# Routing and expert products of a gated cross-attention and expert kernel: GpSimd takes over normalising and adding, products leave PSUM in fours

## The reference

```
for layer in (0, 1):
    x = x + tanh(g_xattn[layer]) * attention(layernorm(x), ctx, ctx [, mask])
    x = x + tanh(g_ffn[layer])   * experts(layernorm(x))
# experts, layer 0 (512 hidden features an expert):
    g = softmax(x @ gate_w);   top 2 of 8, divided by their sum
    y[e] = gelu(x @ w1[e] + b1[e]) @ w2[e] + b2[e];   out = sum over the top 2 of g * y
# experts, layer 1 (64 hidden features an expert):
    g = sigmoid(x @ gate_W) * route_scale;   top 2 of 8, divided by their sum
    the same, plus a shared expert gelu(x @ Ws1 + bs1) @ Ws2 + bs2
```

## Time and profile before

| | |
|---|---|
| median of three runs | 1082.89 us |
| the profiled execution | 1076.07 us, its span 1074.2 us |
| busy: PE / DVE / ACT / POOL | 940.6 / 770.7 / 587.4 / 459.4 us (88 / 72 / 55 / 43%) |
| chain that ended last | PE 63%, DVE 20%, ACT 8%, issue 5%, SP queue 2% |
| mean granted TensorE clock | 0.973 |

### The profile page before, as it was taken

How to read it: one execution, slowest core, us unless ns; L and a number is a source line. 1 busy time by engine, 2 the same in 40 slices (tenths; PEclk the granted TensorE clock), 3 DMA queues, 4 the chain that set the end, 5 groups by cost and what they waited for, 6 DMA issues and landing times.

```text
span 1074.2 us, 32336 instructions
## 1 busy us (share of the span) xinstructions
PE 940.6 (88%) x13088; PEld 687.4 (64%) x13088; DVE 770.7 (72%) x1691; ACT 587.4 (55%) x1068; POOL 459.4 (43%) x573
## 2 busy tenths in 40 slices
PE   2487898999989899898999989898989999998974
PEld 0154577777777677676777767666666666665753
DVE  3376585886768778686885868788787878787723
ACT  1044546555565554656546565565757565656550
POOL 5353435432434333343435464464646465552000
PEclk9998899999999999999999999999999999999985
DMA  8645652332313333133454756757575667666200
GB/s 176 127 87 132 141 129 63 74 77 66 76 38 83 68 75 74 32 83 68 92 131 67 157 102 130 156 119 152 120 150 106 147 116 157 126 133 103 41 16 3
DMA packets 95216, 107.26 MB, mean 100 GB/s; under 512 B 22394, under 2 KB 86972, under 8 KB 95068
## 3 DMA queue, kind: packets, MB, share of 16 engines
q1 hardware_dynamic: 95068, 105.19, 47.6%
HBM read 35.89 MB, written 0.46 MB: 34 GB/s over the span
## 4 chain that ended last, share of the span: by engine, by line
PE 63%; DVE 20%; ACT 8%; issue 5%; SPq 2%; DMA 1%; POOL 0%; POOLq 0%; DVEq 0%; ACTq 0%
PE pO L976 13%; PE pMX L993 12%; PE pST L955 10%; DVE mx L913 6%; PE pFY L1091 5%; PE pKV L1041 5%; PE pFH L1115 5%; PE pKV L1034 5%; DVE mx L904 5%; ACT P L641 3%; DVE rden L807 2%; PE pFY L1058 2%; ACT L641 1%; PE pFY L1095 1%; ACT HR L678 1%
## 5 line engine op out<-in xcount | busy, mean ns | idle before, releaser
L641 ACT ACTIVATE P<-pST 125x448 f32<-125x448 f32 x768 | 396.5, 542 | 379.0 <-PE pST L955 372.2
L913 DVE TENSOR_REDUCE mx<-pMX 112x1 f32<-112x500 f32 x384 | 258.4, 673 | 135.1 <-PE pMX L993 134.6
L993 PE MATMUL pMX<-kop,qmax 104*112 104x500 f16 x768 | 295.0, 394 | 46.9 <-DMA qmax<-qlo 21.5
L955 PE MATMUL pST<-qexp,kop 106*128 106x112 f16 (+1 forms) x3072 | 280.9, 215 | 15.8 <-issue 9.1
L955 PEld LDWEIGHTS pST<-qexp,kop 106*128 106x128 f16 (+1 forms) x3072 | 209.9, 102 | 123.9 <-issue 45.4
L904 DVE TENSOR_REDUCE mx<-pMX 112x1 f32<-112x500 f32 x384 | 255.8, 666 | 29.5 <-PE pMX L993 26.8
L976 PE MATMUL pO<-P,V 125*17 125x112 f32 x6144 | 187.8, 263 | 0.0
L976 PEld LDWEIGHTS pO<-P,V 125*17 125x17 f32 x6144 | 138.2, 98 | 48.0 <-issue 36.1
L551 POOL CAST khi<-kfull 128x500 f16<-128x500 f32 x96 | 58.9, 613 | 246.5 <-ACT kfull L654 246.0
L993 PEld LDWEIGHTS pMX<-kop,qmax 104*112 104x112 f16 x768 | 99.3, 132 | 99.7 <-DVE mx L913 24.0
L553 POOL TENSOR_TENSOR klo<-kfull,khi 128x500 f16<-128x500 f32 x96 | 109.0, 1135 | 7.7
(11 more groups left out here) (143 smaller groups left out, 1120.0 us busy)
## 6 DMA issues: line engine op xcount, KB each, us to landing
C<-in_ctxT SPq DMA_DIRECT2D x32, 750.0 KB, 6.0
kop<-khi SPq DMA_DIRECT2D x192, 125.0 KB
kop<-maskop SPq DMA_DIRECT2D x48, 437.5 KB
kop<-klo SPq DMA_DIRECT2D x96, 125.0 KB
qexp<-qmax SPq DMA_DIRECT2D x32, 182.0 KB
...
qmax<-qhi SPq DMA_DIRECT2D x128, 7.0 KB
```

What stands on the lines that cost most here:

```text
L641: nc.scalar.activation(P[0:KP, slot, h * 4 * T:(h + 1) * 4 * T], pST[0:KP, h, 0:4 * T], ACT.Exp, scale=EXP_SCALE).then_inc(exp_done, 1)
L913: nc.vector.tensor_reduce(mx[:, s % 2, m // PAIRS, m % PAIRS:m % PAIRS + 1], pMX[0:T, 1, 0:CW], AX.X, ALU.max).then_inc(max_done, 1)
L955: mm = nc.tensor.matmul(pST[0:cols, h, i * T:(i + 1) * T], kop[0:ROWS, b, p, tile * KP:tile * KP + cols], qexp[0:ROWS, b, p, :, :].rearran ...
L993: nc.tensor.matmul(pMX[0:T, m % 2, 0:CW], qmax[0:SHIFT0, st.s % 2, p, :, :].rearrange("r j q -> r (j q)"), kop[0:SHIFT0, st.s % 2, p, c * ...
```

## The change

- `fy_uses`: y0 and y1 go to kt 10 and 11, y2 and y3 to kt 1 and 2 of the odd step, yb to kt 4. y0 and y1 fill the four 128-column parts of `pFY`, and so do y2 and y3; only the second of each pair is emptied and releases the bank.
- One VectorE instruction multiplies four products by their four gates (`ysc`). GpSimd adds the eight in odd steps, between chunk 0 and chunk 1 of the keys. VectorE adds yb and the residual in one instruction and the sum in another.
- GpSimd computes `xnq` and `xnf` after its roots.
- The top two come from the eight-largest instruction and a replacement of the two values by zero; layer 0 no longer divides by the softmax's sum (it cancels).
- `ones` shares `xnfT`'s memory, and the attention output is scaled in place.

```diff
     if has_end(s):
-        uses += [(1, "y3", 1), (3, "yb", 1)]
+        uses += [(1, "y2", 0), (2, "y3", 1), (4, "yb", 1)]
     if has_f(s):
-        uses += [(7, "gT", 1)] + [(9 + i, f"y{i}", 1) for i in range(3)]
+        uses += [(7, "gT", 1)] + [(10, "y0", 0), (11, "y1", 1)]
+def columns_of(e):
+    return slice(D * (e % 4), D * (e % 4 + 1))
...   GpSimd, at the start of an odd step (has_q), after rkq
+                    nc.gpsimd.tensor_scalar(xnq[:, :], xg((s + 1) // 2), mvq[:, 0:1], rkq[:, :],
+                                            ALU.subtract, ALU.mult).then_inc(xnq_done, 1)
                 low_part(st, 0)
                 mask_part(st, 0)
+                if has_end(s):
+                    pool.wait_ge(fy_free, upto(fy_uses, s - 1, "y1", True))
+                    y0, y1 = ysc[:, 0, 0:2, :], ysc[:, 1, 0:2, :]
+                    link(nc.gpsimd.tensor_tensor(y0, y0, ysc[:, 0, 2:4, :], ALU.add))
+                    pool.wait_ge(fy_free, upto(fy_uses, s, "y3", True))
+                    link(nc.gpsimd.tensor_tensor(y1, y1, ysc[:, 1, 2:4, :], ALU.add))
+                    link(nc.gpsimd.tensor_tensor(y0, y0, y1, ALU.add))
+                    nc.gpsimd.tensor_tensor(acc[:, 1, :], ysc[:, 0, 0, :], ysc[:, 0, 1, :], ALU.add).then_inc(ysum_done, 1)
                 low_part(st, 1)
...   GpSimd, after low_part(st, 2), after rsf (has_a)
+                    nc.gpsimd.tensor_scalar(xnf[:, :], XF[:, :], mvf[:, 0:1], rsf[:, :],
+                                            ALU.subtract, ALU.mult).then_inc(xnf_done, 1)
...   VectorE
                     elif use == "yb":
-                        nc.vector.tensor_tensor(acc[:, 0, :], pFY[0:T, 0:D], acc[:, 1, :], ALU.add).then_inc(fy_free, 1)
-                        nc.vector.scalar_tensor_tensor(out=xg(lambda s: (s - 5) // 2), in0=acc[:, 0, :],
-                                                       scalar=gains[0:T, 2 + l:3 + l], in1=XF[:, :],
+                        nc.vector.scalar_tensor_tensor(out=acc[:, 0, :], in0=pFY[0:T, 0:D], scalar=gains[0:T, 2 + l:3 + l],
+                                                       in1=XF[:, :], op0=ALU.mult, op1=ALU.add).then_inc(fy_free, 1)
+                        dve.wait_ge(ysum_done, end_count(s) + 1)
+                        nc.vector.scalar_tensor_tensor(out=xg((s - 5) // 2), in0=acc[:, 1, :],
+                                                       scalar=gains[0:T, 2 + l:3 + l], in1=acc[:, 0, :],
                                                        op0=ALU.mult, op1=ALU.add).then_inc(x_done, 1)
+                    elif use in ("y1", "y3"):
+                        k = int(use[1]) // 2
+                        nc.vector.tensor_tensor(ysc[:, k, :, :], pFY[0:T, 0:4 * D].rearrange("t (e d) -> t e d", e=4),
+                                                gate[:, 4 * k:4 * k + 4].unsqueeze(2).broadcast_to([T, 4, D]),
+                                                ALU.mult).then_inc(fy_free, 1)
...   VectorE, shares(kt), with p = ge in layer 0 and gp in layer 1
                     if kt == 2:
-                        nc.vector.tensor_tensor(ggt[:, :, :], pj, pe_, ALU.is_gt)
-                        link(nc.vector.tensor_tensor(geq[:, :, :], pj, pe_, ALU.is_equal))
-                        link(nc.vector.tensor_tensor(gel[:, :, :], geq[:, :, :], before_me[:, :, :], ALU.mult))
+                        link(nc.vector.max(out=top[:, :], in_=p[:, :]))
+                        link(nc.vector.tensor_copy(top2[:, 0:2], top[:, 0:2]))
                     if kt == 3:
+                        link(nc.vector.match_replace(out=rest[:, :], in_to_replace=top2[:, :], in_values=p[:, :], imm_value=0.0))
                     if kt == 4:
+                        link(nc.vector.tensor_tensor(gden[:, :], top[:, 0:1], top[:, 1:2], ALU.add))
+                        link(nc.vector.tensor_tensor(gsp[:, :], p[:, :], rest[:, :], ALU.subtract))
...   TensorE
+                            if l == 1 and i % 2:
+                                pe.wait_ge(fy_ready, upto(fy_uses, s, f"y{i - 1}"))
```

More of the change, by code:

```diff
@@ L190, in links, with pool_links @@
     if has_f(s):
-        n += 9 + (layer_of(s - 3) == 1) + 2
+        n += 6 + 3 * (layer_of(s - 3) == 1)
+    return n
+def pool_links(s):
+    n = 0
+    if has_q(s):
+        n += 3
+    if is_batch(s - 2):
+        n += 1
+    if has_a(s):
+        n += 2
     if has_end(s):
-        n += 2
+        n += 3
     return n
@@ L317, in build @@
         HR = sb("HR", [128, E0 * F0C, T])
+        ysc = sb("ysc", [T, 2, 4, D])
         acc = sb("acc", [T, 2, D])
@@ L529, in _, with links_before @@
                                     pattern=[[-32, 4], [0, 32]], channel_multiplier=1).then_inc(init_p, 1)
-            nc.gpsimd.affine_select(out=before_me[:, :, :], in_=before_me[:, :, :], compare_op=ALU.is_gt, fill=0.0,
-                                    base=0, pattern=[[1, NE], [-1, NE]], channel_multiplier=0).then_inc(init_p, 1)
-            linked = [0]
-            def link(ins):
-                linked[0] += 1
-                ins.then_inc(pool_link, 1)
-            def pool_links(s):
-                return sum(2 * has_q(t) + is_batch(t - 2) + has_a(t) for t in range(-1, s))
+            def links_before(s):
+                return sum(pool_links(t) for t in range(-1, s))
             def low_part(st, c):
@@ L574, in step @@
-                    nc.gpsimd.tensor_tensor(rkq[:, :], rsq[:, :], keep[:, :], ALU.mult).then_inc(rstdq_done, 1)
+                        pool.wait_ge(keep_done, mask_count(s) + 1)
+                        apart(pool)
+                    link(nc.gpsimd.tensor_tensor(rkq[:, :], rsq[:, :], keep[:, :], ALU.mult))
+                    if s >= 1:
+                        pool.wait_ge(fh_ready, upto(fh_uses, s - 2, "qT"))
+                        apart(pool)
+                    nc.gpsimd.tensor_scalar(xnq[:, :], xg((s + 1) // 2), mvq[:, 0:1], rkq[:, :],
+                                            ALU.subtract, ALU.mult).then_inc(xnq_done, 1)
@@ L593, in step @@
                 low_part(st, 2)
+                if has_a(s):
+                    pool.wait_ge(statf_done, a_count(s) + 1)
+                    apart(pool)
+                    link(nc.gpsimd.tensor_scalar(vef[:, :], mvf[:, 1:2], EPS, None, ALU.add))
+                    link(nc.gpsimd.tensor_tensor(rsf[:, :], vef[:, :], mhalf[:, :], ALU.pow))
+                    if s >= 5:
+                        pool.wait_ge(fy_ready, upto(fy_uses, s - 2, "xT"))
+                        apart(pool)
+                    nc.gpsimd.tensor_scalar(xnf[:, :], XF[:, :], mvf[:, 0:1], rsf[:, :],
+                                            ALU.subtract, ALU.mult).then_inc(xnf_done, 1)
                 if has_mask(s):
-                    pool.wait_ge(mask_in, st.at(lambda s: 16 * (maskraw_count(s) + 1)))
+                    pool.wait_ge(mask_in, 16 * (maskraw_count(s) + 1))
                     apart(pool)
@@ L598, in step @@
                                             ).then_inc(mask_done, 1)
-                if has_a(s):
-                    n = 2 * has_q(s) + 2
-                    pool.wait_ge(statf_done, st.at(lambda s: a_count(s) + 1))
-                    apart(pool)
-                    nc.gpsimd.tensor_scalar(vef[:, :], mvf[:, 1:2], EPS, None, ALU.add).then_inc(pool_link, 1)
-                    pool.wait_ge(pool_link, st.at(lambda s: pool_links(s) + n))
-                    nc.gpsimd.tensor_tensor(rsf[:, :], vef[:, :], mhalf[:, :], ALU.pow).then_inc(rstdf_done, 1)
+                assert linked[0] == pool_links(s), (s, linked[0], pool_links(s))
                 if s <= NB - 3:
@@ L905, in step @@
                                                 pMX[0:T, 0, 0:CW], AX.X, ALU.max).then_inc(max_done, 1)
-                    if has_a(s) and kt == 9:
-                        dve.wait_ge(rstdf_done, st.at(lambda s: a_count(s) + 1))
-                        nc.vector.tensor_scalar(xnf[:, :], XF[:, :], mvf[:, 0:1], rsf[:, :],
-                                                ALU.subtract, ALU.mult).then_inc(xnf_done, 1)
                     if has_m(s):
@@ L926, in step @@
                                                 ).then_inc(keep_done, 1)
-                    if has_q(s) and kt == 3:
-                        dve.wait_ge(rstdq_done, st.at(lambda s: q_count(s) + 1))
-                        nc.vector.tensor_scalar(xnq[:, :], xg(lambda s: (s + 1) // 2), mvq[:, 0:1], rkq[:, :],
-                                                ALU.subtract, ALU.mult).then_inc(xnq_done, 1)
                 assert linked[0] == links(s), (s, linked[0], links(s))
```

101 lines of the change are left out of this document (42 added, 59 removed).

## The result

The changed kernel takes 1150.87 us (median of four runs, 1149.92 to 1154.42) where the kernel before, run beside it, takes 1081.9. The ratio is 1.065 (95%: 1.061 to 1.069). It is slower, as forecast, but by 69 us and not by 23, and outside the range. The profiled execution has a span of 1149.8 us at a mean granted clock of 0.922, where before had 1074.2 at 0.973. The two profiled spans differ by 75.6 us and not by 69, since the profiled execution of before was one of its quick ones (1076.07 us).

A forecast was written before the change was run, and what follows sets the result against it. TensorE's in-order queue was taken as the limit. Layer 0's terms of 12.0 us, +11 for the clock, +1.2 for GpSimd waits, +0.5 for layer 1 and -1.5 for the tail gave +23: 1106 us from 1082.89, range 1090 to 1119.

The forecast's parts named there:

- y0 and y1 moved: Layer-0 even steps, kt 9 to 10: TensorE idles 4.3 us until ScalarE's exponential; one uncovered group adds 1.81 us a period.
- The clock, layer 0: After layer 0's Gelu gaps: 7 of 8 bring half speed at 2.0 us each, against 3 at 1.0 now; +11 us.
- VectorE's evacuation: Eight 0.35 us product instructions a period become two of 0.70; VectorE saves 1.4 us, none on layer 0's path.
- the wait at kt 5: Odd steps: yb's two instructions precede xnqT, keepT and OM, delaying the sum matmul; with yb's move, +0.56 us a layer-0 period.
- Normalising on GpSimd: xnq and xnf on GpSimd at 0.5 us each (bounds 0.25 and 0.7); xnf's transpose starts earlier, -0.46 us a layer-0 period.
- Top two: VectorE at kt 2: three comparisons of 0.9 us become 0.45, so the load of w1a waits less; -0.41 us a layer-0 period.
- the waits of short VectorE instructions behind GpSimd: Port pair shared by GpSimd and some VectorE instructions: new adds lengthen waits of short SBUF instructions; left at nothing.
- Adds on GpSimd: Odd steps, 2.6 us of additions; VectorE waits only in steps 15 to 29, 0.4 us in three layer-0 pairs (+1.2), 1.1 in layer 1's five.
- Layer 1: Gelu gap of some 1.8 us, y3's 0.62, the GpSimd wait and VectorE savings: +0.5 us together, bounds -1.5 and +1.5 a period.
- GpSimd rival: GpSimd becomes the bound: dearer forms or blocking make VectorE wait for the sum in nearly every odd step; 1119 us, chance 0.12.
- Tail: Last step: four rounds of group, two VectorE instructions and wait become two pairs; net -1.5 us.

The follow-up runs named there:

- filler: The changed kernel plus 18 (layer 0) or 9 (layer 1) overwritten 512-column matmuls ahead of the scores of kt 10: 1106.15 us, ratio 1.023.
- slots_alone: The kernel before with only the new slots for y0 to y3 and yb, products, sum and normalising staying on VectorE: 1135.13 us, ratio 1.048.
- sum_first: The changed kernel with GpSimd's four additions moved ahead of khi, klo and maskop of chunk 0: 1117.97 us, ratio 1.035.
- early2_filler: The changed kernel, product groups at kt 9 to 11, yb at kt 3, additions starting GpSimd's odd step, overwritten matmuls (8 or 4) ahead of y0: 1059.29 us, ratio 0.980.
- top2_alone: The kernel before with only the new top two (eight-largest, copy, replacement, subtraction): 1082.3 us, ratio 1.001.
- back_and_first: The changed kernel with y0 and y1 back at kt 9 and 10, and GpSimd's four additions ahead of chunk 0 of the keys: 1090.54 us, ratio 1.010.
- early2: The changed kernel with all four product groups at kt 9 to 11, yb at kt 3, additions at the start of GpSimd's odd step: 1070.15 us, ratio 0.990.
- y0_back: The changed kernel with y0 and y1 one slot earlier, at kt 9 and 10, nothing else undone: 1104.4 us, ratio 1.020.

## Why the prediction was right, and where it was wrong

**y0 and y1 moved: right in layer 0.** Forecast was a gap of 4.3 us ended by ScalarE, measured 4.46; and +1.81 uncovered. With the clock held at 1.00 (filler) the period is 67.3 against 65.5. That is +1.8 for all of layer 0's terms together, where the prediction had 1.81 + 0.56 - 0.46 - 0.41 = 1.5.

**The clock, layer 0: right in kind, a little small.** 7 falls of 2.0 us were taken. All eight gaps have one, and filler, which keeps the clock up, shortens the seven periods of the table from 488.3 to 472.6 us together: 2.2 each. With all its terms layer 0's eight periods were forecast 24 us longer, and they are 32 us longer. The gaps of the kernel before that the prediction calls 2.1 us long are 2.21. The rule of the Trainium skill ("TensorE: Matmul & The Clock Gate", "HAM oscillation"), that a recurring gap brings the clock down anew each time, agrees with the trace here: behind every one of them the clock fell.

**VectorE's evacuation: the size right, the saving without use, the wait at kt 5 too small.** The wide multiplication took 0.691 us (taken 0.70). slots_alone, which lacks it, has nearly the same layer-0 periods as the changed kernel (69.5 to 71.1 against 68.8 to 71.0, on average 0.6 us longer, where xnf alone was to bring 0.46), so the eight small instructions were worth next to nothing there, as said. For the sum matmul behind `X`, `xnqT`, `keepT` and `OM` the prediction had +0.56 a period. TensorE's waits there (total us, times, longest), before:

```profile
PE pFY L1052 <- DVE OM L898: 4.4, 15, 0.6
```

In slots_alone:

```profile
PE pFY L1052 <- DVE OM L898: 11.4, 29, 1.2
```

In the changed kernel:

```profile
PE pFY L1068 <- DVE OM L920: 25.9, 29, 2.1
```

In sum_first:

```profile
PE pFY L1068 <- DVE OM L920: 19.4, 29, 1.3
```

In early2_filler, with yb at kt 3 again, it is 8.1 us in 15 waits, as in top2_alone.

Later slots add 7.0 us over 16 periods, 0.44 each, close to the 0.56. With the rest of the change it is 15.0 even without the wait for the sum (sum_first), 0.94 each. The new top two is part of that: alone it raises these waits from 4.4 to 8.3 us (top2_alone). The instruction that writes `X` was taken as 0.35 us. It takes 0.35 wherever GpSimd is idle beside it, 0.49 to 0.66 in the 13 steps of the changed kernel in which GpSimd's `khi` runs beside it (see its 0.57 above, and GpSimd's cast, which follows the sum at once), and up to 1.2 in sum_first, beside `klo` or `maskop`. These waits account for what back_and_first still has over before in layer 0 (66.3 against 65.4 us in periods without a fall, with 0.6 to 0.9 us more of them). In layer 1 they are 1.4 us more a period while the period is 0.6 longer (57.7 against 57.1), so other terms give 0.8 back there.

**Normalising on GpSimd: the price was wrong.** Taken 0.5, upper bound 0.7, measured 0.808 (both forms). The bound came from a mask row of 1500 columns and one-column forms; a form with two operands from the partition's scalars has no neighbour among those rows. The wait itself went as told, but was smaller than priced: in the row at 472.71 of the earlier trace rows TensorE had stood 0.32 us, so no more than 0.32 could be gained there, and not 0.46. TensorE's waits for `xnf`, before and after:

```profile
PE pFY L1062 <- DVE xnf L908: 8.4, 13, 3.0
```

```profile
PE pFY L1078 <- POOL xnf L636: 3.6, 1, 3.6
```

Twelve waits of 0.32 to 0.72 us are gone, and the one in the last group became longer. As time the gain has its sign shown only together with xnq: layer-0 periods of 64.6 to 66.1 in early2, 64.7 to 67.1 with both back on VectorE.

**Top two: wrong, by nothing for the total.** Forecast -0.41 a layer-0 period, measured 0 (ratio 1.001). After, on VectorE:

```profile
L888 DVE COPY top<-top 112x2 f32<-112x2 f32 x16 | 8.2, 511 | 0.6
...
L887 DVE MAX8 top<-gp 112x8 f32<-112x8 f32 x8 | 1.3, 161 | 0.1
```

The eight-largest costs 0.16 as estimated. The two-column copy, taken as 0.15, costs 0.17 where GpSimd is idle and 0.56 behind its cast (top2_alone, above). The last of the three comparisons, which the prediction read as a 0.50 instruction, did the same: 0.22 us in the last two groups, 0.50 in the other 14. So before and after, kt 2's small instructions end right behind GpSimd's `khi` (0.08 and 0.02 us), and a lighter set of them ends no sooner unless it is through before the cast begins. The step that failed is the one that the prediction left at nothing, the waits of short VectorE instructions behind GpSimd: 0.39 us a copy, 0.40 a subtraction, and 0.1 to 0.3 in front of `X`.

**Adds on GpSimd: the wait right, its consequence missed.** Additions of 0.725 and 0.456 us (taken 0.71 and 0.49). Waits only from step 15 on: three of 0.66 us and five of 1.44, 9.2 us, where 3 x 0.4 + 5 x 1.1 = 6.7 was taken, and one of 0.4 in the last group. Plain steps don't wait. So far the mechanism was as told.

**Layer 1: the step that failed.** The prediction saw both causes, "without y0 the gap becomes one of some 1.8 us" (measured 1.95) and the GpSimd wait, and priced them as time waited: +0.5 us for layer 1, at most 1.5 a period. It let the clock fall in layer 0 alone, and put the falls of layer 1 at nothing without a reason, though in its own rows three gaps of 2.2 us in eight had a fall behind them. Layer 1's five periods came out 35 us longer. Runs that differ in one thing, with periods that have or lack a fall, take the +7.6 us of a period apart, to within 0.1:

| part of 64.7 - 57.1 us | read from | us |
|---|---|---|
| fall behind the Gelu gap | 64.7 against filler's 60.8 | 3.9 |
| fall behind the wait at kt 5 | y0_back's 60.4 against its 58.8 | 1.6 |
| VectorE's wait for the sum itself | y0_back's 58.8 against back_and_first's 57.7 | 1.1 |
| y0 gone from the Gelu gap, without a fall | sum_first's 58.2 against back_and_first's 57.7 | 0.5 |
| all else | 57.7 against 57.1 | 0.6 |

The wait for the sum is what the prediction took (1.1), and 5.5 of 7.6 us are the two falls that it left out. filler is the plainest of these runs: it adds only useless work, takes 4.2 of 6.5 points away over both layers, and brings layer 1's five periods from 319.8 to 302.5 us. The GpSimd rival named in the prediction (1119) is a part of the answer: with the sum early 3.0 of the 6.5 points go (sum_first), and GpSimd's lateness matters more by bringing the clock down than by the time waited.

**Tail: no gain.** -1.5 forecast, +9.3 measured from 974.2 on. 5.0 of that lie in the period called next (49.0 to 54.0), which has a Gelu gap of 1.95 us and 10 us at the lower level behind it, as in layer 1; back_and_first has 49.5 there. The other 4.3 lie in the last stretch, here for before, top2_alone and after:

```profile
1023.30:1074.20 50.90, 29.62 (x329) 21.57 (x321) 16.16 (x47) 14.49 (x27) 3.42 (x6) 0.66 0.04 10
1022.40:1076.80 54.40, 34.10 (x329) 24.70 (x329) 15.74 (x46) 14.52 (x27) 3.42 (x6) 0.57 0.04 9
1094.50:1149.80 55.30, 33.77 (x329) 24.50 (x321) 12.55 (x33) 14.46 (x27) 9.48 (x15) 0.58 0.04 9
```

top2_alone, with the old tail but for its top two, takes 54.4 us there, so most of those 4.3 us are the clock that before's profiled execution happened to get, and not the change. The forecast gain of 1.5 doesn't show; the tail was not tested by itself.

**Open.** Why gaps of the same length at the same place bring the clock down in one period and not in another: the Gelu gaps of 1.94 and 1.95 us, five of six with a fall in the changed kernel and one of six in sum_first, and the waits of 2.06 us in y0_back, three of five. What TensorE did before the gap may differ between them, but no run varied that alone. Of the 15.0 us by which the waits for `OM` grow in sum_first, the later slots alone make 7.0 and the new top two alone 3.9; how the other 4.1 divide between the dearer `X` and the order around it wasn't separated.
